# A GEGLU layer with a quantized down projection: the up projection as seven block products a tile instead of eight, its low weight parts streamed

## The chip, the cores and the metric

One Trainium2 chip, one core. The metric is the device time of one execution in microseconds (us). The core has TensorE (PE; its weight loads are shown as PEld), VectorE (DVE), ScalarE (ACT), GpSimd (POOL) and SyncE (SP), which here issues all transfers. Each engine works its own instructions in order; semaphores order the engines among each other.

## The reference

`x` is 4 x 1024 x 512 float32, `cond` 4 x 128, `norm_w` 512 x 128, `up_w` 4096 x 512, `down_w` 512 x 2048.

```python
scale = cond @ norm_w.T + 1.0
ms = jnp.mean(x * x, axis=-1, keepdims=True)
h = x * (scale[:, None, :] * jax.lax.rsqrt(ms + EPS))
val, gate = jnp.split(h @ up_w.T, 2, axis=-1)
h = val * jax.nn.gelu(gate, approximate=False)
y = act_quant(h) @ weight_quant(down_w).T     # h to 255 levels by the row's largest |h|; down_w to -1, 0, 1 by its mean |w|
return y + x
```

## The kernel before

The 4,096 rows of `x` are worked in NB = 8 blocks of TB = 512 rows, the 2,048 hidden columns in J = 16 tiles of 128. All of it is transposed: hidden columns on the partitions, rows of `x` as columns of the matmul. A tile of a block is one step of the up projection. float32 accuracy comes from two float16 parts of each operand, high and low, and three products a pass: high by high, high weight by low x, low weight by high x (lines 257 to 259).

**PE.** `gate` and `val` call `up_half`: 4 slices of the contraction (KT) by 3 products of 512 columns, each into its own bank of `ps_u`. A tile is 24 products. In block b, PE also does the row maxima of block b-1 (`turn_max`, four transposes into `ps_m`), the spread of its scale (`spread_scale`, into `ps_s`), the spread of the next block's reciprocal root (`spread_rs`), and the down products of block b-1 in four groups of 16 (`down`, line 305) after tiles 8 to 11.

**ACT.** `gelu` of the gate bank into `g` (L394), `absolute` of the finished `h` into the same buffer (L400), squares of the next block's rows (L410), x high parts (`high`, L418), and in block 0 `weight_bound` (largest |w| of a tile, L427), `weight_high` (`w_hi`, L432) and `sum_down` (L439).

**DVE.** `hidden` (L612) is `h = val * g`; `peak_of` (L625) keeps the running maximum; `quantize` scales h (L650) and rounds it to `q` (L655); `residual` (L662) scales the down product and adds x; `norm` (L595) and `low` (L602) make the next block's x; `rsqrt` (L564 to L579) is a chain of small operations; in block 0 `weight_scale` (L536 to L546) and `weight_low` (`w_lo`, L553).

**POOL.** Block 0: a reduction over the partitions for each tile's weight scale (L510). Then the quantized down weights `dw` (L524 to L528).

**SP and the transfers.** Up weights come in once, through four stages `w_raw`, and stay on chip in two float16 parts for all tiles, 1,024 columns each a tile. Rows of x stay in `xr`, three blocks deep; the residual is written into them and stored from there.

The order of each engine's work is written out by hand. Block 0 is written out tile by tile, as in this part of DVE's order:

```python
for j in range(J):
    if j + 2 < J:
        weight_scale(j + 2, j % 2)
    if j >= 1:
        peak_of(0, j - 1, (j - 1) % 2, first=True)
    if j + 2 < J:
        weight_low(j + 2, j % 2)
    hidden(0, j, j % 2, first=True)
```

Blocks 1 to 6 are a loop of the hardware, block 7 and the tail are written out again. In the tail `last_down` (L364) goes tile by tile behind the quantization of block 7, which DVE and ACT share (L767, L771, L495, L497).

## Time and profile before

| | |
|---|---|
| median of 3 runs | 814.78 us (814.5 to 814.89) |
| span of the profiled execution | 813.9 us |
| PE busy | 791.4 us |
| PEld busy | 363.4 us |
| DVE busy | 419.8 us |
| ACT busy | 258.8 us |
| POOL busy | 36.4 us |
| moved by DMA | 42.42 MB |

The profile is of one execution; its span is the time from the first to the last instruction, and the table's first row includes what lies around it. Busy is the sum of the durations; PE's matmuls overlap in the profile (each is shown as 0.38 us while one starts each 0.22 us), so the share says where PE is without work, not how fast it is. The chain of work that ended last goes back from the last instruction, at each step to what released it.

### The profile page before, as it was taken

What the parts mean: (1) busy time and instruction counts of PE and PEld (TensorE: products, weight loads), DVE (VectorE), ACT (ScalarE), POOL (GpSimd) and SP (SyncE); (2) the same over time, 40 slices, a digit from 0 to 9 for tenths busy, and PEclk for the clock granted to TensorE, in tenths of its full rate; (3) what the DMA queues carried; (4) which work ended last, traced back from release to release, by engine and by line L of the source; (5) the groups of instructions that cost most, each with busy time, mean ns of one, the idle gap of its engine ahead of it and who ended that gap; (6) DMA issues with size and microseconds to landing.
All of it is one profiled execution on the core that took longest, in us unless ns stands there. A gap on an engine that the chain in (4) does not pass through costs nothing.

```text
span 813.9 us, 12449 instructions
## 1 busy us (share of the span) xinstructions
PE 791.4 (97%) x3688; PEld 363.4 (45%) x3688; DVE 419.8 (52%) x830; ACT 258.8 (32%) x430; POOL 36.4 (4%) x48
## 2 busy tenths in 40 slices
PE   1999999999999999999999999999999999999997
PEld 1444444444444444444444444444444444444443
DVE  4667778433664426743376334664346633563237
ACT  3887623222232122322232221322223222221224
POOL 0100076000000000000000000000000000000000
PEclk9999999999999999999999999999999999999999
DMA  7744530003000030001100030000300010000002
GB/s 271 257 157 155 201 106 4 14 26 117 0 0 13 33 110 0 0 26 60 68 0 0 26 122 7 0 0 26 129 0 0 0 39 13 1 0 14 13 5 74
DMA packets 11825, 42.42 MB, mean 52 GB/s; under 512 B 1440, under 2 KB 1440, under 8 KB 9760
## 3 DMA queue, kind: packets, MB, share of 16 engines
q1 hardware_dynamic: 11808, 42.21, 14.3%
q8 instruction: 8, 0.13, 0.1%
q14 instruction: 9, 0.07, 0.0%
HBM read 33.82 MB, written 8.39 MB: 52 GB/s over the span
## 4 chain that ended last, share of the span: by engine, by line
PE 95%; DVE 3%; issue 1%; ACT 0%; DMA 0%; POOL 0%; SPq 0%; DVEq 0%; ACTq 0%
PE ps_u L257 27%; PE ps_u L258 27%; PE ps_u L259 27%; PE ps_y L305 11%; DVE h L767 1%; PE ps_m L283 1%; PE ps_s L290 0%; PE ps_m L298 0%; PE ps_u L364 0%; DMA scaled<-in_norm_t_dram 0%; DVE w_raw L771 0%; DVE h_max L625 0%; PE ps_y L344 0%; DVE h L612 0%; DVE xr L662 0%
## 5 line engine op out<-in xcount | busy, mean ns | idle before, releaser
L257 PE MATMUL ps_u<-x_hi,w_hi 128*128 (+1 forms) x1024 | 389.1, 380 | 3.4 <-DVE x_lo L602 3.4
L258 PE MATMUL ps_u<-x_lo,w_hi 128*128 (+1 forms) x1024 | 389.1, 380 | 0.0
L259 PE MATMUL ps_u<-x_hi,w_lo 128*128 (+1 forms) x1024 | 389.1, 380 | 0.0
L612 DVE SCALAR_TENSOR_TENSOR h<-ps_u,w_unscale,g 128x512 f32<-128x512 f32 (+1 forms) x128 | 96.0, 750 | 276.0 <-PE ps_u L259 274.6
L400 ACT ACTIVATE g<-h 128x512 f32 (+1 forms) x128 | 80.6, 630 | 335.9 <-DVE h L612 335.9
L257 PEld LDWEIGHTS ps_u<-x_hi,w_hi 128*128 (+1 forms) x1024 | 100.3, 98 | 123.5 <-DVE w_lo L553 3.8
L259 PEld LDWEIGHTS ps_u<-x_hi,w_lo 128*128 (+1 forms) x1024 | 100.4, 98 | 121.5 <-issue 1.1
L258 PEld LDWEIGHTS ps_u<-x_lo,w_hi 128*128 (+1 forms) x1024 | 100.4, 98 | 118.5 <-issue 0.6
L394 ACT ACTIVATE g<-ps_u,w_unscale 128x512 f32<-128x512 f32 x128 | 87.4, 683 | 178.8 <-PE ps_u L259 176.4
L305 PE MATMUL ps_y<-dw,q 128*128 128x512 bf16 x448 | 101.4, 379 | 0.0
L625 DVE TENSOR_TENSOR h_max<-g,h_max 128x512 f32<-128x512 f32 x120 | 83.9, 699 | 32.6 <-ACT g L400 32.6
L650 DVE TENSOR_TENSOR scaled<-h,ps_s 128x512 f32<-128x512 f32 x112 | 71.5, 680 | 10.1 <-PE ps_s L290 10.1
L305 PEld LDWEIGHTS ps_y<-dw,q 128*128 128x128 bf16 x448 | 43.9, 98 | 52.4
L655 DVE TENSOR_SCALAR q<-scaled 128x512 bf16<-128x512 f32 (+1 forms) x112 | 46.6, 459 | 0.0
L602 DVE TENSOR_TENSOR x_lo<-xn,x_hi 128x512 f32 (+1 forms) x32 | 22.0, 691 | 26.9 <-ACT x_hi L418 26.8
L553 DVE SCALAR_TENSOR_TENSOR w_lo<-w_raw,w_scale,w_hi 128x1024 f16<-128x1024 f32 x16 | 20.6, 1284 | 15.5 <-ACT w_hi L432 15.5
L595 DVE SCALAR_TENSOR_TENSOR xn<-xt_raw,cs,ps_m 128x512 f32<-128x512 f32 x32 | 23.5, 740 | 0.7 <-PE ps_m L298 0.7
L432 ACT ACTIVATE w_hi<-w_raw,w_scale 128x1024 f16<-128x1024 f32 x16 | 18.3, 1143 | 14.8 <-DVE w_scale L540 14.8
L662 DVE SCALAR_TENSOR_TENSOR xr<-ps_y,dequant,xr 128x512 f32 (+1 forms) x28 | 20.9, 746 | 2.6 <-PE ps_y L305 2.6
L418 ACT CAST x_hi<-xn 128x512 f32 (+1 forms) x32 | 19.7, 617 | 5.0 <-DVE xn L595 2.8
L427 ACT ACTIVATE q<-w_raw 128x1024 bf16<-128x1024 f32 x16 | 16.7, 1044 | 0.0
L298 PE MATMUL ps_m<-ident,rs 128*128 128x128 f32 x32 | 5.3, 292 | 10.0 <-DVE rs L579 10.0
(62 smaller groups left out, 193.9 us busy)
## 6 DMA issues: line engine op xcount, KB each, us to landing
xr<-in_x_rows_dram SPq DMA_DIRECT2D x8, 1024.0 KB, 6.4
w_raw<-in_up_t_dram SPq DMA_DIRECT2D x16, 512.0 KB, 4.2
xt_raw<-in_x_cols_dram SPq DMA_DIRECT2D x8, 1024.0 KB, 5.4
out_dram<-xr SPq DMA_DIRECT2D x32, 256.0 KB, 2.5
xr<-in_down_t_dram SPq DMA_DIRECT2D x8, 512.0 KB, 4.2
w_raw<-in_down_t_dram SPq DMA_DIRECT2D x8, 512.0 KB, 4.4
scaled<-in_norm_t_dram SPq DMA_DIRECT2D x1, 256.0 KB, 2.8
cond_sb<-in_cond_t_dram SPq DMA_DIRECT2D x1, 2.0 KB, 1.6
```

The source lines that it names most:

```text
L257: pe.matmul(bank, w_hi[:, w_at], x_hi[:, x_at], start=(kt == 0), stop=False)
L258: pe.matmul(bank, w_hi[:, w_at], x_lo[:, x_at], start=False, stop=False)
L259: last = pe.matmul(bank, w_lo[:, w_at], x_hi[:, x_at], start=False, stop=(kt == KT - 1))
L305: last = pe.matmul(ps_y[:, i % 2, :], q[:, j * TB + i * P:j * TB + (i + 1) * P], dw[:, j * D:(j + 1) * D], start=(j == 0), stop=(j == J - 1))
L394: act.activation(g[:, s, :], ps_u[:, 2 * s + 1, :], ACT.Gelu, scale=w_unscale[:, ds(j, 1)]).then_inc(g_ready, 1)
L400: act.activation(g[:, s, :], h[:, ds(j * TB, TB)], ACT.Abs).then_inc(h_abs_ready, 1)
L595: dve.scalar_tensor_tensor(out=xn[:, kt % 2, :], in0=xt_raw[:, kt * TB:(kt + 1) * TB], scalar=cs[:, ds(kt * B + b // PER_B, 1)], in1=ps_m[ ...
L602: dve.tensor_tensor(x_lo[:, at], xn[:, kt % 2, :], x_hi[:, at], ALU.subtract).then_inc(x_lo_ready, 1)
L612: dve.scalar_tensor_tensor(out=h[:, at], in0=ps_u[:, 2 * s, :], scalar=w_unscale[:, ds(j, 1)], in1=g[:, s, :], op0=ALU.mult, op1=ALU.mult) ...
L625: dve.tensor_tensor(h_max[:], g[:, s, :], h_max[:], ALU.max).then_inc(h_max_ready, 1)
L650: dve.tensor_tensor(scaled[:, s, :], h[:, ds((t + s) * TB, TB)], ps_s[:], ALU.mult).then_inc(scaled_ready, 1)
L655: dve.tensor_scalar(q[:, ds((t + s) * TB, TB)], scaled[:, s, :], ROUND, ROUND, ALU.add, ALU.subtract).then_inc(q_ready, 1)
```

## The change

The x block of 512 rows and the contraction of 512 are each halved, and so are the two halves (value and gate) of a weight tile; the 2 x 2 block product is done with Strassen's scheme in Winograd's form: seven block products of 2 slices by 3 passes by 256 columns (`product`), 42 a tile. The operands are A11, A12, A22 and four sums S1 to S4 of weight blocks, and B11, B21, B22 and four differences of x blocks.

- Weight sums: `weight_sums` on POOL, four operations of 128x256, for each tile in block 0. `w_hi` and `w_lo` of a tile are 1,792 columns wide.
- `w_hi` stays on chip for all tiles. `w_lo` is a ring of LS = 4 tiles: written in block 0, stored to DRAM (`store_lo`), and loaded again for each tile of blocks 1 to 7 (`load_lo`, three tiles ahead).
- Two stages instead of four for the up weights (the first lies in `q`) and for the down weights.
- x: `norm` in place in `xt`, four `difference` operations, and seven high and seven low parts of 512 columns where there were four.
- Sums of the products: ACT's `copies` takes the first pair of a tile out of its bank (one half to the gate bank `ps_g`, one to `p5`), DVE's `seed_gate` adds the second product into the gate bank, and `second_val` adds the third into the value bank. Products accumulate on top.
- The order on PE: first pair of tile n; third and both gate products of tile n-1; second of tile n; fourth of tile n-1. So a tile is finished in the step after its own. ACT and DVE follow with hidden, absolute and peak of tile n-2.
- `ps_m` serves maxima, scales and roots alike, `ps_s` is gone; the banks are three for values, two for gates, two for the down product.
- Down products of block b-1: the first group after tile 15 of block b, the other three in tiles 0 to 2 of block b+1. Quantization of a block is spread over tiles 3 to 14 of the next, two, one, one tile of h at a step.
- Rows of x for the squares and for the residual are loaded apart, in pieces of 128 rows, into two buffers each (`xs`, `res`); a result is stored from `res` before the buffer is loaded again.
- All 128 tiles are written out, with no loop of the hardware. `X_TOP` is 2^8 instead of 2^10.

```diff
-            def up_half(b, j, s, which, as_ready=False):
-                    pe.matmul(bank, w_hi[:, w_at], x_hi[:, x_at], start=(kt == 0), stop=False)
-                    pe.matmul(bank, w_hi[:, w_at], x_lo[:, x_at], start=False, stop=False)
-                    last = pe.matmul(bank, w_lo[:, w_at], x_hi[:, x_at], start=False, stop=(kt == KT - 1))
...
+            def load_up(j):
+                if j >= 2:
+                    sp.wait_ge(w_ready, j - 1)
+                sp.dma_start(stage[j % 2][:, 0:WJ], up_t[j]).then_inc(up_loaded[j % 2], 16)
+
+            def store_lo(j):
+                sp.wait_ge(w_ready, j + 1)
+                sp.dma_start(lo_dram[j], w_lo[:, (j % LS) * WO:(j % LS + 1) * WO]).then_inc(lo_stored[j % LS], 16)
+
+            def load_lo(n):
+                j = n % J
+                sp.wait_ge(val_ready, n - LS + 1)
+                sp.wait_ge(lo_stored[n % LS], 16 * (J // LS))
+                sp.dma_start(w_lo[:, (n % LS) * WO:(n % LS + 1) * WO], lo_dram[j]).then_inc(lo_loaded[n % LS], 16)
...
+            def load_res(c, i):
+                u = y_tile(c, i)
+                if u >= 2:
+                    sp.wait_ge(y_stored[u % 2], 16 * (u // 2))
+                sp.dma_start(res[:, u % 2, :], x_rows[c][:, i * D:(i + 1) * D]).then_inc(res_loaded[u % 2], 16)
+
+            def store_y(c, i):
+                u = y_tile(c, i)
+                sp.wait_ge(y_done, u + 1)
+                sp.dma_start(out[c][:, i * D:(i + 1) * D], res[:, u % 2, :]).then_inc(y_stored[u % 2], 16)
...
+                if j == 0 and 1 <= b < NB - 1:
+                    load_xt(b + 1)
+                for c in range(1, NB):
+                    for i in range(TT):
+                        if xs_tile(c, i) >= 2 and n == squares_at(c, i) - 1:
+                            load_xs(c, i)
+                if b >= 1 and j in (12, 13):
+                    load_res(b - 1, j - 12)
+                if b >= 2 and j < 4:
+                    if j in (1, 2):
+                        load_res(b - 2, j + 1)
+                    store_y(b - 2, j)
+                if n + 3 >= J and n + 3 < NJ:
+                    load_lo(n + 3)
+            for i in range(TT):
+                if i in (1, 2):
+                    load_res(NB - 2, i + 1)
+                store_y(NB - 2, i)
+            for i in range(TT):
+                if i < 2:
+                    load_res(NB - 1, i)
+            for i in range(TT):
+                store_y(NB - 1, i)
+                if i < 2:
+                    load_res(NB - 1, i + 2)
+            for k in range(2):
+                sp.wait_ge(y_stored[k], NB * TT // 2 * 16)
...
+            def product(n, op, xop, bank, half, start=False):
+                b, j = divmod(n, J)
+                if j == 0:
+                    pe.wait_ge(x_hi_ready, NOP * b + xop + 1)
+                    pe.wait_ge(x_lo_ready, NOP * b + xop + 1)
+                to = bank[:, half * HB:(half + 1) * HB]
+                for kt in range(2):
+                    wh = ((j * NOP + op) * 2 + kt) * P
+                    wl = (((n % LS) * NOP + op) * 2 + kt) * P
+                    xa = (((b % 2) * NOP + xop) * 2 + kt) * HB
+                    hi, lo = x_hi[:, xa:xa + HB], x_lo[:, xa:xa + HB]
+                    pe.matmul(to, w_hi[:, wh:wh + P], hi, start=start and kt == 0, stop=False, skip_group_check=True)
+                    pe.matmul(to, w_hi[:, wh:wh + P], lo, start=False, stop=False, skip_group_check=True)
+                    last = pe.matmul(to, w_lo[:, wl:wl + P], hi, start=False, stop=(kt == 1), skip_group_check=True)
+                return last
+
+            def first_pair(n):
+                b, j = divmod(n, J)
+                if b == 0:
                     pe.wait_ge(w_ready, j + 1)
+                else:
+                    pe.wait_ge(lo_loaded[n % LS], 16 * ((n - J) // LS + 1))
+                if n >= NV:
+                    pe.wait_ge(h_ready, n - NV + 1)
+                bank = ps_v[:, n % NV, :]
+                product(n, OA11, XB11, bank, 0, start=True)
+                product(n, OS1, XT1, bank, 1).then_inc(pair_ready, 1)
+
+            def second(n):
+                pe.wait_ge(pair_copied, 2 * (n + 1))
+                product(n, OS2, XT2, ps_v[:, n % NV, :], 0).then_inc(u2_ready, 1)
+
+            def third(n):
+                pe.wait_ge(g_seeded, n + 1)
+                product(n, OS3, XT3, ps_v[:, n % NV, :], 0).then_inc(u3_ready, 1)
+
+            def gates(n):
+                bank = ps_g[:, n % NG, :]
+                product(n, OA12, XB21, bank, 0)
+                product(n, OS4, XB22, bank, 1).then_inc(gate_ready, 1)
+
+            def fourth(n):
+                pe.wait_ge(v2_ready, n + 1)
+                product(n, OA22, XN4, ps_v[:, n % NV, :], 0).then_inc(val_ready, 1)
+
+            def spread_rs(c):
+                pe.wait_ge(rs_ready, c + 1)
+                if c >= 1:
+                    pe.wait_ge(xn_ready, c * KT)
+                if c >= 3:
+                    pe.wait_ge(scaled_ready, (c - 2) * J)
+                for i in range(TT):
+                    last = pe.transpose(ps_m[:, i * P:(i + 1) * P], rs[:, i:i + 1].to_broadcast([P, P]), ident[:])
+                last.then_inc(rs_rows, 1)
...
+                pe.wait_ge(xn_ready, min(b + 3, NB) * KT)
+                pe.wait_ge(scaled_ready, b * J)
...
+            for n in range(NJ + 1):
+                b, j = divmod(n, J)
+                if n < NJ:
+                    first_pair(n)
+                if n >= 1:
+                    third(n - 1)
+                    gates(n - 1)
+                if n < NJ:
+                    second(n)
+                if n >= 1:
+                    fourth(n - 1)
+                if n == NJ:
+                    break
+                if 1 <= b and j == 2:
+                    spread_scale(b - 1)
+                for c in range(1, NB):
+                    if n == spread_rs_at(c):
+                        spread_rs(c)
+                if b >= 2 and j < 3:
+                    down(b - 2, j + 1)
+                if b >= 1 and j == J - 1:
+                    down(b - 1, 0)
+                if 1 <= b and j == 1:
+                    turn_max(b - 1)
+
+            down(NB - 2, 1)
+            down(NB - 2, 2)
             turn_max(NB - 1)
+            down(NB - 2, 3)
             spread_scale(NB - 1)
+
+            banks = [ps_v[:, 0, :], ps_v[:, 1, :], ps_v[:, 2, :], ps_g[:, 0, :]]
...
+            def copies(n):
+                act.wait_ge(pair_ready, n + 1)
+                if n >= NG:
+                    act.wait_ge(g_ready, n - NG + 1)
+                act.copy(ps_g[:, n % NG, 0:HB], ps_v[:, n % NV, 0:HB]).then_inc(pair_copied, 1)
+                if n >= 2:
+                    act.wait_ge(v2_ready, n - 1)
+                act.copy(p5[:, n % 2, :], ps_v[:, n % NV, HB:TB]).then_inc(pair_copied, 1)
...
+            for n in range(NJ + 2):
+                b, j = divmod(n, J)
+                if n < NJ:
+                    copies(n)
+                if n >= 2:
+                    absolute(n - 2)
+                if 1 <= n < NJ + 1:
+                    gelu(n - 1)
+                if b == 0:
+                    if j + 2 < J:
+                        weight_high(j + 2)
+                    if j + 3 < J:
+                        weight_bound(j + 3)
+                    if j == 12:
+                        high(1, XB11)
+                        high(1, XT1)
+                        high(1, XT2)
+                    if j == 13:
+                        high(1, XT3)
+                    if j == 14:
+                        high(1, XB21)
+                        high(1, XB22)
+                        high(1, XN4)
+                if 1 <= b < NB - 1:
+                    if j == 2:
+                        high(b + 1, XB11)
+                        high(b + 1, XT1)
+                        high(b + 1, XT2)
+                        high(b + 1, XT3)
+                    if j == 3:
+                        high(b + 1, XB21)
+                        high(b + 1, XB22)
+                        high(b + 1, XN4)
+                for c in range(1, NB):
+                    for i in range(TT):
+                        if n == squares_at(c, i):
+                            square(c, i)
+                if J - 1 <= n < J + 3:
+                    sum_down(2 * (n - J + 1))
+                    sum_down(2 * (n - J + 1) + 1)
...
+            def weight_sums(j):
+                part = [stage[j % 2][:, k * 2 * P:(k + 1) * 2 * P] for k in range(8)]
+                a21, a22, a11, a12, s1, s2, s3, s4 = part
+                pool.wait_ge(up_loaded[j % 2], (j // 2 + 1) * 16)
+                pool.tensor_tensor(s1, a21, a22, ALU.add).then_inc(s_step, 1)
+                pool.tensor_tensor(s3, a11, a21, ALU.subtract).then_inc(s_step, 1)
+                pool.wait_ge(s_step, 4 * j + 1)
+                pool.tensor_tensor(s2, s1, a11, ALU.subtract).then_inc(s_step, 1)
+                pool.wait_ge(s_step, 4 * j + 3)
+                pool.tensor_tensor(s4, a12, s2, ALU.subtract).then_inc(s_step, 1)
...
+            def seed_gate(n):
+                dve.wait_ge(u2_ready, n + 1)
+                dve.tensor_tensor(ps_g[:, n % NG, HB:TB], ps_v[:, n % NV, 0:HB], p5[:, n % 2, :],
+                                  ALU.add).then_inc(g_seeded, 1)
+
+            def second_val(n):
+                dve.wait_ge(u3_ready, n + 1)
+                dve.tensor_tensor(ps_v[:, n % NV, HB:TB], ps_v[:, n % NV, 0:HB], p5[:, n % 2, :],
+                                  ALU.add).then_inc(v2_ready, 1)
...
+            for n in range(NJ + 2):
+                b, j = divmod(n, J)
+                if 1 <= b < NB and j == 2:
+                    row_scales(b - 1)
+                if b == 0 and j + 2 < J:
+                    weight_scale(j + 2)
+                if n >= 2:
+                    hidden(n - 2)
+                if 1 <= n < NJ + 1:
+                    second_val(n - 1)
+                if n >= 2:
+                    peak_of(n - 2)
+                if b >= 2 and j < 4 and n < NJ:
+                    residual(b - 2, j, ps_y[:, j % 2, :])
+                k = j - Q_FIRST
+                tiles = []
+                if 1 <= b < NB and 0 <= k < len(Q_COUNT):
+                    tiles = Q_ORDER[sum(Q_COUNT[:k]):sum(Q_COUNT[:k + 1])]
+                for t in tiles:
+                    scaled(b - 1, t)
+                if n < NJ:
+                    seed_gate(n)
+                for t in tiles:
+                    rounded(b - 1, t, q)
+                if b == 0:
+                    if j + 2 < J:
+                        weight_low(j + 2)
+                    if j == 10:
+                        norm(1, 0)
+                        norm(1, 1)
+                    if j == 11:
+                        norm(1, 2)
+                        norm(1, 3)
+                    if j == 12:
+                        difference(1, XT1)
+                        difference(1, XT2)
+                    if j == 13:
+                        low(1, XB11)
+                        difference(1, XT3)
+                        low(1, XT1)
+                    if j == 14:
+                        difference(1, XN4)
+                        low(1, XT2)
+                        low(1, XT3)
+                    if j == 15:
+                        low(1, XB21)
+                        low(1, XB22)
+                        low(1, XN4)
+                if b == 1 and j == 3:
                     dve.wait_ge(d_summed, ND)
                     dve.tensor_reduce(d_sum[:], d_sums[:], AX.X, ALU.add).then_inc(d_sum_ready, 1)
+                if b == 1 and j == 4:
                     dve.wait_ge(d_total_ready, 1)
                     dve.tensor_scalar(d_mean[:], d_total[:], 1.0 / (J * P * D), CLIP, ALU.mult,
                                       ALU.max).then_inc(d_step, 1)
                     dve.wait_ge(d_step, 1)
                     dve.reciprocal(d_scale[:], d_mean[:]).then_inc(d_scale_ready, 1)
+                if 1 <= b < NB and j == 5:
+                    row_dequant(b - 1)
+                if 1 <= b < NB - 1:
+                    if j == 1:
+                        for kt in range(KT):
+                            norm(b + 1, kt)
+                    if j == 2:
+                        difference(b + 1, XT1)
+                        difference(b + 1, XT2)
+                        low(b + 1, XB11)
+                        difference(b + 1, XT3)
+                        low(b + 1, XT1)
+                        difference(b + 1, XN4)
+                    if j == 15:
+                        for k in (XT2, XT3, XB21, XB22, XN4):
+                            low(b + 1, k)
+                for c in range(1, NB):
+                    if n == rsqrt_at(c):
+                        rsqrt(c)
+
+            residual(NB - 2, 0, ps_y[:, 0, :])
+            residual(NB - 2, 1, ps_y[:, 1, :])
             residual(NB - 2, 2, ps_y[:, 0, :])
+            row_scales(NB - 1)
+            row_dequant(NB - 1)
+            residual(NB - 2, 3, ps_y[:, 1, :])
             for j in range(J):
+                scaled(NB - 1, j)
                 if j % 2 == 1:
+                    rounded(NB - 1, j - 1, q_last)
+            banks = [ps_v[:, 0, :], ps_v[:, 1, :], ps_v[:, 2, :], ps_g[:, 0, :]]
             for i in range(TT):
...
```

## Rows read from the trace of the kernel before

**Rows 1.** The page: busy time by engine, and the chain that ended last by engine

```profile
PE 791.4 (97%) x3688; PEld 363.4 (45%) x3688; DVE 419.8 (52%) x830; ACT 258.8 (32%) x430; POOL 36.4 (4%) x48
...
PE 95%; DVE 3%; issue 1%; ACT 0%; DMA 0%; POOL 0%; SPq 0%; DVEq 0%; ACTq 0%
```

**Rows 2.** Windows of block 0 and the tail: stretch, its us, busy us of each engine

```profile
20.30:106.40 86.10, 86.09 (x389) 38.59 (x390) 57.66 (x133) 65.32 (x105) 7.18 (x18) 1.00 0.51 183
786.90:813.90 27.00, 22.30 (x105) 10.07 (x103) 19.44 (x37) 10.71 (x17) 0.00 (x0) 1.00 0.16 59
```

**Rows 3.** The chain in order of time: start us, us, what

```profile
154.94 3.45 PE ps_y L305 x16
...
305.89 0.65 PE ps_m L283 x4
...
404.14 0.65 PE ps_m L283 x4
...
793.17 1.29 DVE h L767 x2
```

**Rows 4.** Timeline of PE and its weight loads around a group of transposes

```profile
443.70 0.57 PEld L298 LDWEIGHTS ps_m<-ident,rs 128*128 128x128 f32 x4
443.92 0.60 PE L298 MATMUL ps_m<-ident,rs 128*128 128x128 f32 x4
...
444.36 0.38 PE L257 MATMUL ps_u<-x_hi,w_hi 128*128 x1
```

**Rows 5.** The page's groups of instructions: xcount | busy us, mean ns | idle before, releaser

```profile
L612 DVE SCALAR_TENSOR_TENSOR h<-ps_u,w_unscale,g 128x512 f32<-128x512 f32 (+1 forms) x128 | 96.0, 750 | 276.0 <-PE ps_u L259 274.6
L400 ACT ACTIVATE g<-h 128x512 f32 (+1 forms) x128 | 80.6, 630 | 335.9 <-DVE h L612 335.9
L257 PEld LDWEIGHTS ps_u<-x_hi,w_hi 128*128 (+1 forms) x1024 | 100.3, 98 | 123.5 <-DVE w_lo L553 3.8
...
L394 ACT ACTIVATE g<-ps_u,w_unscale 128x512 f32<-128x512 f32 x128 | 87.4, 683 | 178.8 <-PE ps_u L259 176.4
...
L625 DVE TENSOR_TENSOR h_max<-g,h_max 128x512 f32<-128x512 f32 x120 | 83.9, 699 | 32.6 <-ACT g L400 32.6
...
L553 DVE SCALAR_TENSOR_TENSOR w_lo<-w_raw,w_scale,w_hi 128x1024 f16<-128x1024 f32 x16 | 20.6, 1284 | 15.5 <-ACT w_hi L432 15.5
...
L432 ACT ACTIVATE w_hi<-w_raw,w_scale 128x1024 f16<-128x1024 f32 x16 | 18.3, 1143 | 14.8 <-DVE w_scale L540 14.8
```

**Rows 6.** Timeline of DVE and ACT: a reciprocal root, and one tile of block 0

```profile
13.34 0.17 DVE L564 TENSOR_SCALAR ms<-sumsq 128x4 f32<-128x4 f32 x1
...
15.61 0.15 DVE L536 TENSOR_SCALAR peak_all<-peak_all 128x1 f32<-128x1 f32 x1
...
38.29 1.28 DVE L553 SCALAR_TENSOR_TENSOR w_lo<-w_raw,w_scale,w_hi 128x1024 f16<-128x1024 f32 x1 [1.46 <-ACT w_hi L432]
...
39.50 0.74 DVE L612 SCALAR_TENSOR_TENSOR h<-ps_u,w_unscale,g 128x512 f32<-128x512 f32 x1
...
41.85 1.13 ACT L432 ACTIVATE w_hi<-w_raw,w_scale 128x1024 f16<-128x1024 f32 x1
...
43.08 1.28 DVE L553 SCALAR_TENSOR_TENSOR w_lo<-w_raw,w_scale,w_hi 128x1024 f16<-128x1024 f32 x1 [1.45 <-ACT w_hi L432]
```

**Rows 7.** POOL: its group of reductions, and two single operations of the timeline

```profile
L510 POOL PARTITION_ALL_REDUCE peak_all<-peak x16 | 6.3, 391 | 78.0 <-ACT q L427 78.0
...
105.19 1.10 POOL L524 TENSOR_SCALAR w_raw<-w_raw,d_scale 128x1024 f32<-128x1024 f32 x1 [9.58 <-issue]
...
123.08 1.80 POOL L524 TENSOR_SCALAR w_raw<-w_raw,d_scale 128x1024 f32<-128x1024 f32 x1
```

**Rows 8.** The page's DMA issues: xcount, KB each, median us from issue to landing

```profile
w_raw<-in_up_t_dram SPq DMA_DIRECT2D x16, 512.0 KB, 4.2
...
out_dram<-xr SPq DMA_DIRECT2D x32, 256.0 KB, 2.5
...
scaled<-in_norm_t_dram SPq DMA_DIRECT2D x1, 256.0 KB, 2.8
```

718 lines of the change are left out of this document (319 added, 399 removed).

## The prediction

> **What bounds the kernel now.** I read the summary by engine first. TensorE is busy 97% of the span, and the chain that ended last lies on PE for 95% [rows 1]. So PE's own instructions, their number and their spacing, make the time. The windows cut the 813.9 us into three pieces: 20.3 us before the first up product, 766.6 us up to 786.9, where the last up product ends (block 0 is 86.1 of them, up to 106.4, and blocks 1 to 7 are the other 680.5), and a tail of 27.0 us [rows 2]. The chain in order of time gives the spacing: sixteen down products of 512 columns take 3.45 us, 0.2157 us each, and from one block's transposes of the row maxima to the next block's are 98.25 us [rows 3]. That is 384 up products (82.83 us), 64 down products (13.80) and 1.6 us of transposes with their gaps. Nothing else fits in: in the middle blocks PE never waits. DVE is busy 52% and ACT 32% [rows 1], so they have room, but not without limit.
>
> **Fewer columns.** A tile had 24 products of 512 columns and gets 42 of 256: 12,288 columns become 10,752. The catch is that each product still loads 128x128 weights, and there are now 5,376 of them where there were 3,072. At 2.4 GHz 512 columns are 0.2133 us, so 0.0024 us of the 0.2157 is a fixed part of each product; 256 columns are then 0.1067 + 0.0024 = 0.1091 us. A load takes 0.098 us [rows 5] and starts with the product ahead of it, so it would just be covered. The nearest row: four transposes with a load each start at 443.92 and the next product at 444.36, 0.11 us a pair, loads included [rows 4]. I take 0.1091. The bounds: half of 0.2157, 0.1078 (7 us less in all); 0.11 from the transposes (5 us more); and load and stream one after the other, 0.206, which those transposes make unlikely. A tile costs 42 x 0.1091 = 4.58 us instead of 5.18, and 128 tiles save 76 us if nothing else is late. The rest of the working is what is late.
>
> The Trainium skill, "TensorE: Matmul & The Clock Gate", sections on the wait of 56 ns and on the back-to-back gap, has a fixed 2.5 ns per product, which the trace's 0.2157 agrees with. The same page says that pairs of load and product do not get below 81 ns, which would leave my 0.109 alone, but also that the sequencer, when it decodes in software, spends 62 ns per matmul; if a load costs it the same, a pair is 0.124 us and the sum 80 us higher. The pair of 0.11 in the trace speaks against it, over four pairs only.
>
> **One tile in the new order.** From the tile's start on PE (0): first pair to 1.31, third and gates of the tile before to 3.27, second to 3.93, fourth of the tile before to 4.58. An operation of 256 columns isn't in the trace. DVE's 512 columns take 0.70 to 0.75, ACT's 0.63 to 0.68, and the 1,024-column rows give 1.04 and 1.03 ns a column [rows 5]; so 256 columns are 0.45 on DVE and 0.38 on ACT (bounds: half and the whole of the 512-column rows). ACT copies at 1.68 to 2.4, wanted at 3.27. `second_val` goes at 2.33 to 2.8, wanted at 3.93. `seed_gate` waits for second (4.30), ends near 4.75, and in a tile in which two tiles are quantized, near 5.45; wanted by third at 5.89. So steady tiles don't stall, by a margin of 0.4 us.
>
> **Places that stall, blocks 1 to 7.** A Newton reciprocal root is eleven small operations, from 13.34 to 15.61: 2.3 us [rows 6]. Where it comes in a tile without a down product (j=11, blocks 1 to 5), DVE is 0.9 us late for the next seed; j=3 with a residual costs 0.2. So 1.1 us in blocks 2 to 6. Block 1 has no down products in its first tiles to hide things: `spread_rs(2)` waits for a root queued behind that tile's seed (2.7), `turn_max(0)` for four norms of 0.66 each behind the next seed (2.9), and at tile 19 the copies stand on ACT behind four x copies and two sums of down chunks of 1.14 us each [rows 5] (2.6); with the small ones 9.4. All blocks together: 9.4 + 5.5 + 0.2 = 15.1 us. The low parts of the weights, 0.46 MB a tile, take about the 4.2 us of an up load [rows 8] and have two tiles, 9.2 us; I cost them at nothing. That cover is gone only if SyncE stands still for 4 us, which in blocks 2 to 7 I don't find.
>
> **Block 0.** Here the price is. The first product starts at about 21 (20.3 before [rows 2]; the same chain of scales and the root leads to it, with one difference, 0.6, and a low part 0.8 longer on DVE, and squares moved from DVE to ACT, 1.3 less; the rest I round up). What is prepared per tile is 1,792 columns instead of 1,024, in two stages instead of four. ACT's `w_hi` goes from 1.14 to 1.94 us, DVE's `w_lo` from 1.28 to 2.08 [rows 5]. The queues are in order, so this closes a ring (an operation starts up to 0.1 before the one ahead of it ends: `w_lo` at 38.29 takes 1.28, hidden starts at 39.50 [rows 6]): DVE `w_lo` ends; the four scale operations (0.57); hidden (0.75); hand-over (0.12); ACT absolute (0.53); gelu (0.57); `w_hi` 1.94; hand-over (0.10); `w_lo` 2.00 to the next. 6.58 us a tile, against 4.58 on PE and 4.79 from one `w_lo` to the next before, 38.29 to 43.08, `w_hi` ending at 42.98 [rows 6]. A second ring is the stage: load 4.2 [rows 8] plus issue 0.3, `weight_bound` 1.14 (priced as the 1,024 columns of `w_hi`), the reduction over partitions 0.5, gives 6.2: just inside (the reduction itself is 0.39, with hand-overs 0.5 [rows 7]). A third is POOL: four sums of 128x256 after that reduction have 2.9 us until `w_hi` wants them. POOL has no two-input row here; one-input 128x1024 takes 1.10 to 1.80 [rows 7], so a sum is between 0.26 (a quarter) and 1.8. I take 0.5, nearest to the quarter but for two inputs: 2.3 with hand-overs, inside. Since `w_lo` and the POOL sums both read SBUF, and POOL's 1.80 against 1.10 stands beside a working DVE, I add 0.2: 6.8 a tile. At the upper end the sums would add 4.6 a tile, 55 us.
>
> The Trainium skill, "GPSIMD Engine Reference", section on elementwise cycle accounting, gives 4,497 ns for a two-input sum of 2,048 elements; an estimate from that page is 0.56 for 256, and the sum above would stay at 6.8. "SBUF — State Buffer", section "Who interferes with whom", has DVE with two SBUF inputs and GpSimd exclude each other; the trace's 1.80 against 1.10 agrees.
>
> Until the ring runs: two norms, three differences and five low parts (each 0.6 to 0.7) come between the first `w_lo` and the second, so the low part of tile 1 is done at 30.2, of tile 2 at 34.9, of tile 3 (its load waits for tile 1, ACT loads a table) at 42.5. Twelve more at 6.8 are 81.6; the root of x block 1, its four norms and first two differences on the same DVE queue add 2.3 + 2.6 + 1.2. Low part of tile 15: 130.2. Tile 16 starts 8.5 later: 138.7. Before, it was 106.4.
>
> **Tail.** Three groups of down products, 3.45 us each, stand behind the last up product instead of two, and `res` has two buffers. Residual (6,2) waits for a store (2.5) and a load (2.8) [rows 8], then `row_scales` and residual (6,3): the first `scaled` comes 13.3 us after the last product, not 6.2 (793.17 [rows 3] less 786.9); one residual (0.66) is no longer among them. At the very end the rows of (7,2) and (7,3) are loaded only after the stores of (7,0) and (7,1), and SyncE takes them in order: store, load, store, load, store is 12.0 us from the first residual where it was 5.5. So 27.0 + 7.1 - 0.7 + 6.5 = 39.9.
>
> **Sum.** 138.7 to tile 16. Then seven blocks of 16 x 4.58 (513.2), the last third, gates and fourth (2.6), 25 groups of down products (86.3), transposes and their gaps as before (11.0: 680.5 less 579.8 and 26 groups of 3.45), stalls 15.1: 628.2 instead of 680.5. Tail 39.9. 806.8 us of span. The run of before has 814.78 with a span of 813.9, so 0.9 more: 807.7. Saved in blocks 1 to 7: 52; given back: 32 in block 0, 13 in the tail.
>
> **Rivals.** A, the sum as it stands (800 to 813): 0.40. B, block 0 or the stalls are cheaper, as the ring is not closed in each tile (say 6.2 a tile and half the stalls: 793): 0.18. C, the other side: POOL's sums end behind the 2.9 us and the ring is longer. It decides from 7.4 us a tile (7.1 us over 12 tiles); at 8.0 a tile, 822. For it the 1.80 rows, against it the idle POOL: 0.17. D, the steady tiles stall: the margin of 0.4 us is used up by PSUM-to-PSUM operations, which no row shows, and 0.25 us in each of 112 tiles gives 836: 0.10. E, the pair of load and product isn't 0.109: each ns is 5.4 us, so from 0.1104 on the change is slower; at 0.12, 866. Against it the transposes: 0.05. No change that can be told (0.2%, 1.6 us, is about what this kernel's runs can tell): 0.10.
>
> From these: faster 0.58, same 0.10, slower 0.32. The likeliest case's own range is 800 to 813. The range for 8 in 10 leaves out the far ends of POOL's price and of the pair: 790 to 842.
>
> **What would show it.** Starts of up products 0.109 apart; low parts in block 0 6.8 apart, with `w_hi` released by `w_scale` and absolute by hidden, not by POOL; tile 16 at 139; blocks 2 to 6 89.9 us from one turn of the maxima to the next; last up product at 767; tail 40. A released-by-POOL in `w_hi` is C; PE idle before second or third in ordinary tiles is D.

## The result, and the profile after

The changed kernel takes 965.12 us (964.06 to 965.7, 4 runs); beside it the kernel before took 814.84 (814.5 to 815.76). The ratio is 1.184, with an interval of 1.1825 to 1.1859: 18% slower, where 1% faster was forecast. The profiled execution of the changed kernel has a span of 963.3 us, 156.5 more than the 806.8 of the prediction's sum. Two executions that ran at a lower granted clock, one of the kernel before (938.33 us) and one of experiment 7 (982.07 us), are left out of all that follows.

The page after, against [rows 1]: busy time by engine, TensorE's granted clock in 40 slices, and the chain that ended last by engine.

```profile
PE 762.0 (79%) x5966; PEld 607.0 (63%) x5994; DVE 563.0 (58%) x1138; ACT 356.3 (37%) x714; POOL 80.6 (8%) x113
...
PEclk9967676767678999999999999999999999999998
...
PE 60%; issue 23%; POOL 5%; DVE 5%; ACT 3%; DMA 3%; SPq 0%; POOLq 0%; ACTq 0%; DVEq 0%
```

No engine is near its limit any more. The new thing is "issue" with 23% of the chain: time in which the engine on the chain waited for nothing that the profile shows. 23% of 963 is some 220 us. Next, where it lies. Three windows after, cut at the first up product, the start of tile 16, the end of the last up product and the end of the span (stretch, us, busy us of PE, PEld, DVE, ACT, POOL, then the granted clock):

```profile
27.30:288.20 260.90, 115.14 (x652) 80.48 (x653) 85.66 (x170) 80.82 (x132) 47.68 (x75) 0.71 0.24 74
288.20:920.80 632.60, 616.06 (x5186) 511.82 (x5210) 448.04 (x902) 255.67 (x550) 28.20 (x25) 0.99 0.41 132
920.80:963.30 42.50, 26.94 (x119) 12.09 (x119) 20.86 (x39) 10.94 (x18) 0.00 (x0) 0.88 0.27 87
```

| piece | before [rows 2] | predicted | after | after less predicted |
|---|---|---|---|---|
| up to tile 16's first product | 106.4 | 138.7 | 288.2 | +149.5 |
| from there to the end of the last up product | 680.5 | 628.2 | 632.6 | +4.4 |
| tail | 27.0 | 39.9 | 42.5 | +2.6 |

So blocks 1 to 7 and the tail came as forecast, within 1% and 7%, and all but 7 us of the miss lies before tile 16. There PE is busy for 44% of the time, DVE for 33% and POOL for 18%. What ended the waits is in the table of waits of the whole program (us in total, times, longest); nearly all of these lie in block 0:

```profile
PE ps_v L378 <- ACT p L523: 115.6, 17, 12.3
DVE w_lo L716 <- issue: 109.6, 12, 9.7
POOL peak_all L672 <- issue: 90.5, 15, 6.6
...
ACT w_hi L576 <- POOL q L667: 71.5, 8, 14.9
ACT w_hi L576 <- POOL stage L667: 63.9, 8, 11.0
...
POOL q L662 <- issue: 59.7, 8, 9.1
POOL stage L662 <- issue: 58.4, 8, 7.9
```

Read it from the end back to the engine that holds the others up: PE's product `second` waits for ACT's copies, the copies stand in ACT's queue behind `w_hi`, and `w_hi` waits 135.4 us in all for POOL's last sum (L667). That is what the prediction had named as the mark of rival C. But POOL isn't busy. It is itself released by "issue": 15 waits of 6.0 us before the reductions (L672) and 16 of 7.4 before the first sum of a tile (L662). One tile in POOL's timeline:

```profile
137.03 0.71 POOL L662 TENSOR_TENSOR stage<-stage 128x256 f32<-128x256 f32 x1 [7.89 <-issue]
137.72 0.71 POOL L663 TENSOR_TENSOR stage<-stage 128x256 f32<-128x256 f32 x1
...
139.19 0.72 POOL L667 TENSOR_TENSOR stage<-stage 128x256 f32<-128x256 f32 x1
145.87 0.38 POOL L672 PARTITION_ALL_REDUCE peak_all<-peak  x1 [5.96 <-issue]
153.94 0.71 POOL L662 TENSOR_TENSOR q<-q 128x256 f32<-128x256 f32 x1 [7.69 <-issue]
```

Four sums (2.9), 5.96 of nothing, a reduction (0.38), 7.69 of nothing: 16.9 us from tile to tile (16.7 on average over the fifteen steps of the program), and that closes without any other engine. The waits stand only where the kind of work changes. Between sums there is none.

The word "issue" alone proves little. DVE's `w_lo` has 109.6 us of it too, and there it is ACT's `w_hi`, which ends 0.1 us before `w_lo` starts:

```profile
140.01 1.79 ACT L576 ACTIVATE w_hi<-stage,w_scale 128x1792 f16<-128x1792 f32 x1 [8.28 <-POOL stage L667]
141.88 2.08 DVE L716 SCALAR_TENSOR_TENSOR w_lo<-stage,w_scale,w_hi 128x1792 f16<-128x1792 f32 x1 [9.66 <-issue]
```

POOL's operands, in contrast, were there: the maximum that the reduction at 145.87 reads was finished on ACT at 142.84, 3.0 us earlier, and the weights that the sum at 153.94 reads had been read by ACT from 141.70 on. In the kernel before, the reductions followed one another and were released by ACT for 78.0 us [rows 7], which looks like idleness; but at the two places where the kind changes, its table of waits has the same thing:

```profile
POOL peak_all L510 <- ACT q L427: 78.0, 15, 8.8
POOL w_raw L524 <- issue: 9.6, 1, 9.6
POOL peak_all L513 <- issue: 9.0, 1, 9.0
```

L524 is the first scaling of the down weights, behind the last reduction, and its row with [9.58 <-issue] stands in [rows 7]: I took the 1.10 of it and passed over the 9.58. L513 is the first reduction, behind an `affine_select`.

### The profile page after: what moved, and what is told of

The parts are those of the page before. It is cut to its first block, busy times and chain, and to the rows that moved or that the text cites. A ratio compares the mean times of both kernels' runs of the same rounds, so it can differ in the third digit from the quotient of the medians.

```text
span 963.3 us, 15408 instructions
## 1 busy us (share of the span) xinstructions
PE 762.0 (79%) x5966; PEld 607.0 (63%) x5994; DVE 563.0 (58%) x1138; ACT 356.3 (37%) x714; POOL 80.6 (8%) x113
## 4 chain that ended last, share of the span: by engine, by line
PE 60%; issue 23%; POOL 5%; DVE 5%; ACT 3%; DMA 3%; SPq 0%; POOLq 0%; ACTq 0%; DVEq 0%
PE ps_v L378 12%; PE ps_v L380 12%; PE ps_v L379 12%; PE ps_y L444 9%; PE ps_g L379 5%; PE ps_g L380 5%; PE ps_g L378 5%; ACT q L570 2%; DMA out_dram<-res 1%; PE ps_v L494 1%; DVE h L832 1%; DMA res<-in_x_rows_dram 1%; POOL peak_all L672 1%; POOL q L667 1%; POOL q L662 1%
## 5 line engine op out<-in xcount | busy, mean ns | idle before, releaser
L378 PE MATMUL ps_v<-x_hi,w_hi 128*128 128x256 f16 x1280 | 368.7, 288 | 162.1 <-ACT p L523 115.6
L379 PE MATMUL ps_v<-x_lo,w_hi 128*128 128x256 f16 x1280 | 368.7, 288 | 0.0
L380 PE MATMUL ps_v<-x_hi,w_lo 128*128 128x256 f16 x1280 | 368.2, 288 | 0.0
L378 PEld LDWEIGHTS ps_v<-x_hi,w_hi 128*128 128x128 f16 x1280 | 131.5, 103 | 197.4 <-ACT p L523 120.6
L380 PEld LDWEIGHTS ps_v<-x_hi,w_lo 128*128 128x128 f16 x1280 | 132.4, 103 | 21.5
L379 PEld LDWEIGHTS ps_v<-x_lo,w_hi 128*128 128x128 f16 x1280 | 131.7, 103 | 22.1
L378 PE MATMUL ps_g<-x_hi,w_hi 128*128 128x256 f16 x512 | 139.9, 273 | 0.0
L379 PE MATMUL ps_g<-x_lo,w_hi 128*128 128x256 f16 x512 | 139.9, 273 | 0.0
L380 PE MATMUL ps_g<-x_hi,w_lo 128*128 128x256 f16 x512 | 139.7, 273 | 0.0
L797 DVE SCALAR_TENSOR_TENSOR h<-ps_v,w_unscale,g 128x512 f32<-128x512 f32 x128 | 95.5, 746 | 3.0 <-PE ps_v L380 2.8
L780 DVE TENSOR_TENSOR ps_g<-ps_v,p 128x256 f32<-128x256 f32 x128 | 55.0, 429 | 14.7 <-PE ps_v L380 8.0
L716 DVE SCALAR_TENSOR_TENSOR w_lo<-q,w_scale,w_hi 128x1792 f16<-128x1792 f32 x8 | 16.7, 2085 | 72.2 <-issue 54.5
L716 DVE SCALAR_TENSOR_TENSOR w_lo<-stage,w_scale,w_hi 128x1792 f16<-128x1792 f32 x8 | 16.7, 2084 | 71.8 <-issue 55.1
```

Source lines behind the costliest of these rows:

```text
L378: pe.matmul(to, w_hi[:, wh:wh + P], hi, start=start and kt == 0, stop=False, skip_group_check=True)
L379: pe.matmul(to, w_hi[:, wh:wh + P], lo, start=False, stop=False, skip_group_check=True)
L380: last = pe.matmul(to, w_lo[:, wl:wl + P], hi, start=False, stop=(kt == 1), skip_group_check=True)
L780: dve.tensor_tensor(ps_g[:, n % NG, HB:TB], ps_v[:, n % NV, 0:HB], p5[:, n % 2, :], ALU.add).then_inc(g_seeded, 1)
L797: dve.scalar_tensor_tensor(out=h[:, at:at + TB], in0=ps_v[:, n % NV, :], scalar=w_unscale[:, j:j + 1], in1=g[:, n % 3, :], op0=ALU.mult, o ...
```

## The experiments

The theory, S: each change of kind on POOL, between a PARTITION_ALL_REDUCE and a tensor operation, costs 6 to 8 us whatever the size of either, and two changes a tile set the length of block 0. Its main rival is the prediction's C in its own form: the sums are long, or are held up by DVE on SBUF. Four kernels separate these.

**1. The sums on DVE, POOL with reductions alone.** `weight_sums` moves from POOL's queue to DVE's:

```diff
@@ pool
-            def weight_sums(j): ...
             for j in range(J):
-                weight_sums(j)
                 weight_peak_all(j)
@@ dve, ahead of weight_low(j + 2)
+                        weight_sums(j + 2)
```

> The changed kernel with the four weight sums of each tile on DVE instead of POOL, nothing else. Theory S (POOL pays 6 to 8 us each time that its work goes from a sum to a reduction over the partitions or back): POOL now does reductions only, the gaps ahead of them vanish, DVE gets four operations of 0.4 us more a tile, so 8.3 us a tile in block 0 instead of 16.9; about 836 us. Rival R (each reduction over the partitions costs 6 us by itself once POOL has a long queue): the 6 us gap stays, some 13 us a tile, about 910 us. Rival W (two stages and 1,792 columns hold block 0, whatever POOL does): stays at about 960 us.

Measured: 836.6 us, ratio 1.027 (1.024 to 1.029), 128 us less than the changed kernel. POOL's reductions are released by ACT again, and the low parts are 8.11 us apart:

```profile
63.27 1.25 POOL L661 PARTITION_ALL_REDUCE peak_all<-peak  x1 [6.85 <-ACT q L570]
...
62.23 2.08 DVE L715 SCALAR_TENSOR_TENSOR w_lo<-stage,w_scale,w_hi 128x1792 f16<-128x1792 f32 x1 [1.27 <-issue]
...
70.34 2.08 DVE L715 SCALAR_TENSOR_TENSOR w_lo<-q,w_scale,w_hi 128x1792 f16<-128x1792 f32 x1 [1.27 <-issue]
```

This moves both the work and the changes of kind off POOL, so it doesn't yet tell S from long sums. It does show that the ring of the prediction is what is left when POOL's part is gone: its 6.58, without the 0.2 for POOL beside DVE, and the four sums on DVE's queue (1.46 us, from 65.13 to 66.59) are 8.04.

**2. The reductions off POOL, the sums on it.** PE transposes the broadcast column of peaks (as `spread_rs` does) into a bank of `ps_y`, and DVE reduces its 128 columns:

```diff
@@ pe
+            def spread_column(column, ready, count, slot, done):
+                pe.wait_ge(ready, count)
+                pe.transpose(ps_y[:, slot, 0:P], column.to_broadcast([P, P]), ident[:]).then_inc(done, 1)
@@ dve, at the head of weight_scale(j)
+                dve.wait_ge(ready, count)
+                dve.tensor_reduce(to, ps_y[:, slot, 0:P], AX.X, op).then_inc(done, 1)
@@ pool
-                weight_peak_all(j)
```

> The changed kernel with every reduction over the partitions (the scale of cond, 16 weight peaks, the sum of the down weights) taken from POOL and done by a PE transpose of the broadcast column and a DVE reduction of 128 columns; the sums stay on POOL at 0.71 us each. Theory S: no change of kind is left, about 7 us a tile in block 0, tile 16 at 140 us instead of 288, total about 815 us (812 to 825). Rival T (the two-input sums need 7 us ahead of them on POOL by themselves): the gap of 7 us stays ahead of the sums, about 12 us a tile, 880 to 900 us. Rival W: about 960 us.

Measured: 823.69 us, ratio 1.0105 (1.008 to 1.013), a span of 821.5. The expectation was 815 (812 to 825). POOL does the same sixty-four sums as in the changed kernel, and 141 us are gone. So it wasn't the sums' size. POOL's rows, and two low parts 7.27 us apart:

```profile
64.39 1.62 POOL L683 TENSOR_TENSOR stage<-stage 128x256 f32<-128x256 f32 x1 [3.54 <-DMA stage<-in_up_t_dram]
65.97 0.72 POOL L684 TENSOR_TENSOR stage<-stage 128x256 f32<-128x256 f32 x1
...
63.34 2.08 DVE L732 SCALAR_TENSOR_TENSOR w_lo<-q,w_scale,w_hi 128x1792 f16<-128x1792 f32 x1 [1.27 <-issue]
...
70.61 2.08 DVE L732 SCALAR_TENSOR_TENSOR w_lo<-stage,w_scale,w_hi 128x1792 f16<-128x1792 f32 x1 [1.27 <-issue]
```

The first sum is now released by the DMA, and is the only long one of this tile: 1.62 us where the next takes 0.72. From 63.34 to 65.42 `w_lo` runs on DVE. In other tiles it is another of the four that is long, up to 2.51.

**3. The kernel before, with one small sum behind each reduction.** This has none of the change: no Strassen, no sums of weights. The sum is of one column and nothing uses it.

```diff
             for j in range(J):
                 weight_peak_all(j)
+                pool.tensor_tensor(tiny[:, j:j + 1], ident[:, 0:1], ident[:, 1:2], ALU.add)
```

> The kernel before with one sum of 128x1 on POOL behind each of the 16 weight reductions, its result unused. Theory S: the size does not matter, only that the kind changes twice a tile: 6.0 + 0.4 + 7.3 + 0.2, about 14 us a tile in block 0 instead of 5.4; about 950 us. If the price lay in the size of the sums, the two stages or the wide parts: 815 us, as before.

Measured: 958.64 us, ratio 1.176 (1.174 to 1.179). Sixteen operations of 0.18 us, 2.9 us of work in all, make the kernel before 144 us longer (about 135 were expected; two of the waits before a reduction were 7.8 and 9.7):

```profile
65.00 0.18 POOL L518 TENSOR_TENSOR tiny<-ident 128x1 f32<-128x1 f32 x1 [7.19 <-issue]
71.17 0.38 POOL L511 PARTITION_ALL_REDUCE peak_all<-peak  x1 [5.98 <-issue]
79.22 0.18 POOL L518 TENSOR_TENSOR tiny<-ident 128x1 f32<-128x1 f32 x1 [7.68 <-issue]
85.25 0.38 POOL L511 PARTITION_ALL_REDUCE peak_all<-peak  x1 [5.84 <-issue]
```

**4. The changed kernel with its sums cut to one column.** The four sums write one column each; the rest of the sums' part of the stage holds a constant, so the products of those parts aren't those of the reference.

```diff
                 part = [stage[j % 2][:, k * 2 * P:(k + 1) * 2 * P] for k in range(8)]
+                part = [t[:, 0:1] for t in part]
```

> The changed kernel with each of the four weight sums cut to one column of 256; the rest of the sum blocks holds a constant, so the result is not the reference's. Theory S: only the work of the sums goes, 2.8 us down to about 0.6, 14.6 us a tile; about 930 us. If the sums' own work on POOL were the price: block 0 near the 6.8 us a tile of the prediction, about 810 us.

Measured: 929.2 us, ratio 1.140 (1.138 to 1.142). The size of the sums is worth 36 us of the changed kernel's 965, 2.2 us a tile: (0.71 - 0.18) x 4 is 2.1. The waits are as long as before:

```profile
63.80 0.18 POOL L664 TENSOR_TENSOR stage<-stage 128x1 f32<-128x1 f32 x1 [7.26 <-issue]
...
70.29 0.38 POOL L674 PARTITION_ALL_REDUCE peak_all<-peak  x1 [5.74 <-issue]
78.23 0.18 POOL L664 TENSOR_TENSOR q<-q 128x1 f32<-128x1 f32 x1 [7.56 <-issue]
```

With 3 and 4 the price is measured in two kernels and for sums of 1 and of 256 columns: 5.7 to 6.0 us toward the reduction, 7.2 to 7.9 toward the sum in these rows. The wait before a reduction is also the same whether its operand comes late or early: in the changed kernel the maximum is there 2.9 us behind POOL's last sum, in 3 it was there (61.17) 4.0 us before the sum ended (65.18), and the reduction starts 5.96 and 5.98 us behind the sum. S stands, and "long sums" falls.

**5 to 7. What the design is worth without the changes of kind.** Three kernels start from number 2 and go after the two other terms that the prediction had priced: the loads in the tail, and the ring of block 0.

Number 5 loads the rows of x for the last six residuals during block 7, into `xs` and `xt`, which are free by then:

```diff
+            def load_early(c, i):
+                k = y_tile(c, i) - EARLY
+                if k < 2:
+                    sp.wait_ge(sumsq_ready, NB * TT)
+                else:
+                    sp.wait_ge(x_lo_ready, NOP * NB)
+                sp.dma_start(home(c, i), x_rows[c][:, i * D:(i + 1) * D]).then_inc(early_loaded[k], 16)
...
+                if b == NB - 1 and 5 <= j < 11:
+                    u = EARLY + j - 5
+                    load_early(u // TT, u % TT)
```

> The kernel with its reductions off POOL (823.7 us, span 821.5), and in it the rows of x for the last six residuals are loaded during block 7 into tiles that are free by then: (6,2) and (6,3) into the two xs tiles, (7,0) to (7,3) into xt. So no residual waits for a store and a load. T (the terms of the tail as the prediction put them: the last residual no longer two stores and two loads behind, 12.0 back to 5.5 us, and the first scaled about 2 us sooner, since the third residual of block 6 no longer waits for its rows while the third group of down products still does): tail 42.7 - 8.7 = 34, time 815 us (813 to 817). Rival N (the waits on the loads cover something else that is as late: the stores at the end take their time anyway): 821 us or more.

Number 6 opens the ring: a third stage, on ACT `weight_high` and `weight_bound` ahead of `absolute` and `gelu`, on DVE `peak_of` behind `weight_low`, and on PE the peak spread right behind the first pair (not in the lines shown).

```diff
-        stage = [stage0, stage1[:]]
+        stage = [stage0, stage1[:], h[:, 12 * TB:16 * TB]]
@@ act, tile n of block 0
+                    weight_high(j + 2)
+                    weight_bound(j + 3)
                     absolute(n - 2)
                     gelu(n - 1)
-                    weight_high(j + 2)
-                    weight_bound(j + 3)
@@ dve, tile n of block 0
-                    peak_of(n - 2)
                     ...
                     weight_low(j + 2)
+                    peak_of(n - 2)
```

> The kernel with its reductions off POOL, and in block 0: a third stage of raw weights (in the part of h for tiles 12 to 15, which is written only after tile 14's weights are done), each load one tile earlier; ACT does w_hi and the bound of the next tile ahead of absolute and gelu; DVE takes peak_of behind w_lo; PE spreads the peak right behind the first pair. All the instructions stay. R (block 0 is a ring of load and queue order, as the sum of the prediction had it, once POOL no longer changes its kind of work): a tile is then bound by the busier of ACT (copies 0.72, w_hi 1.8, bound 1.25, absolute and gelu 1.3: 5.1 us) and DVE (scales 0.9, hidden 0.75, three of 0.43 to 0.7, w_lo 2.08: 5.3 us), 5.5 us with hand-overs instead of 7.27; over 13 tiles 23 us less: 801 us (797 to 808). Rival N (block 0 is bound by POOL's four sums beside DVE, by DMA or by TensorE's lower clock there): at least 7.0 a tile, 819 to 824.

Number 7 has both edits.

> Both edits: the new order and third stage in block 0, and the rows for the tail early. If they are independent, the time is 823.7 less the sum of what each saves alone: about 792 us (787 to 799), ratio to the kernel before 0.972. If the reductions and the tail were all that stood between the prediction and the change, this is the design as its author could have had it: 52 us saved in blocks 1 to 7, block 0 about 12 us longer than before, tail 7 longer.

| kernel | time, us | ratio to before, interval |
|---|---|---|
| 5, rows early | 812.16 | 0.9967 (0.9957 to 0.9977) |
| 6, third stage and order | 809.2 | 0.9928 (0.991 to 0.9946) |
| 7, both | 796.57 | 0.9768 (0.9747 to 0.9789) |

Number 5 came 1 us below its range, 7 inside its own. 5 saves 11.5 us and 6 saves 14.5; 823.7 less both is 797.7, so the two edits don't get in each other's way. The tail term holds, and a little more than it: in 5 the last up product ends at 777.2 of a span of 808.8, which leaves 31.6 us where number 2 had 42.4 (the expectation's 42.7 puts the last product 0.3 early), so 10.8 less where 8.7 were expected. The last residuals now wait for PE, not for a load. DVE's timeline at the end, of the changed kernel first and of 7 below it:

```profile
929.72 0.75 DVE L847 SCALAR_TENSOR_TENSOR res<-ps_y,dequant,res 128x512 f32<-128x512 f32 x1 [4.51 <-DMA res<-in_x_rows_dram]
...
934.46 1.28 DVE L832 TENSOR_TENSOR h<-h,ps_m 128x512 f32<-128x512 f32 x2
...
949.25 1.61 DVE L847 SCALAR_TENSOR_TENSOR res<-ps_v,dequant,res 128x512 f32<-128x512 f32 x2 [2.46 <-PE ps_v L494]
955.77 0.75 DVE L847 SCALAR_TENSOR_TENSOR res<-ps_v,dequant,res 128x512 f32<-128x512 f32 x1 [4.91 <-DMA res<-in_x_rows_dram]
959.84 0.75 DVE L847 SCALAR_TENSOR_TENSOR res<-ps_g,dequant,res 128x512 f32<-128x512 f32 x1 [3.32 <-DMA res<-in_x_rows_dram]
```

```profile
789.00 2.48 DVE L880 SCALAR_TENSOR_TENSOR xt<-ps_v,dequant,xt 128x512 f32<-128x512 f32 x3 [1.47 <-PE ps_v L529]
791.59 0.75 DVE L880 SCALAR_TENSOR_TENSOR xt<-ps_g,dequant,xt 128x512 f32<-128x512 f32 x1
```

Number 6 missed its expectation by 8 us: 801 were expected, within 797 to 808. Tile 16 starts at 133.1, 16.4 us earlier than in number 2, where 23 were expected. Its first tiles do what was expected of them, and so do those of 7, where the low parts are 5.4 to 6.3 us apart between 52.0 and 80.8. DVE in 7:

```profile
57.90 2.08 DVE L746 SCALAR_TENSOR_TENSOR w_lo<-q,w_scale,w_hi 128x1792 f16<-128x1792 f32 x1 [0.46 <-issue]
...
63.27 2.08 DVE L746 SCALAR_TENSOR_TENSOR w_lo<-stage,w_scale,w_hi 128x1792 f16<-128x1792 f32 x1 [0.46 <-issue]
...
80.79 2.09 DVE L746 SCALAR_TENSOR_TENSOR w_lo<-stage,w_scale,w_hi 128x1792 f16<-128x1792 f32 x1 [0.46 <-issue]
...
83.93 0.69 DVE L755 TENSOR_SCALAR ms<-sumsq 128x4 f32<-128x4 f32 x1
...
91.78 2.09 DVE L746 SCALAR_TENSOR_TENSOR w_lo<-h,w_scale,w_hi 128x1792 f16<-128x1792 f32 x1 [0.20 <-issue]
```

Behind 80.8 the same DVE queue takes the start of x block 1: the root, four norms and two differences, while ACT gets its first x copies. The expectation had spread 5.5 us over all 13 tiles; from tile 10's low part (80.79) to tile 15's (121.19) it is 8.1 a tile. The root itself takes 5.2 us, from 83.93 to 89.1, where [rows 6] had 2.3 for the same operations (they are twelve, not the prediction's eleven): six of them, of 128x4 elements, last 0.56 to 0.69 instead of 0.16, while POOL's sums run. So DVE was the bound there, as named, with work on it that the estimate had left out.

Three windows of 7; the first is cut at 144.0, 11 us behind the start of tile 16:

```profile
21.40:144.00 122.60, 92.78 (x746) 76.15 (x747) 103.88 (x206) 87.46 (x149) 50.05 (x52) 0.96 0.56 172
144.00:763.20 619.20, 606.18 (x5104) 503.96 (x5128) 440.24 (x881) 248.02 (x533) 27.94 (x24) 0.99 0.42 133
763.20:795.10 31.90, 25.73 (x122) 11.86 (x122) 20.85 (x39) 11.28 (x18) 0.00 (x0) 0.99 0.18 67
```

DVE is busy 103.9 of the first 122.6 us (95.8 of the 111.5 up to tile 16), so I expect little more from block 0 without moving work off it; no run tried. Tile 16 starts at 132.9 (26.5 later than before), the last up product ends at 763.5 (23.4 earlier), and the tail is 4.6 longer: 18.8 us of span gained, of the 50 that blocks 1 to 7 give.

## Why the prediction was wrong

**The step that failed** is in the paragraph on block 0: "A third is POOL: four sums of 128x256 after that reduction have 2.9 us until `w_hi` wants them." The sums were priced by their size, between 0.26 and 1.8 us, and the reductions by theirs, 0.39. The order on POOL, reduction, sums, reduction, sums, had no price at all. It costs 6.0 + 7.4 us a tile, so POOL's own ring is 16.7 us and not inside the 6.8. From the end of tile 1's low part to that of tile 15's are 234.5 us (42.8 to 277.3) where the prediction had 100.0 (30.2 to 130.2, with 6.1 for x block 1). The same price (6.78 us before the first sum, then 6.11 and 6.84) stands in the way of the start: the first product is at 27.3, not 21 (21.4 in number 7, without reductions on POOL), and tile 1's low part is 12.6 behind its time. Together with 2.4 us from there to tile 16 that is the 149.5. The bound from above, 1.8 us a sum, could not have held it either, since it was again a size. Rival C had the engine and the sign (0.17), and 8.0 us a tile as its price.

**What number 2 leaves of the miss.** With the changes of kind gone the span is 821.5, 14.7 above the sum. Tile 16 starts at 149.5 there, 10.8 late: the low part of tile 15 ends at 140.5 (130.2 predicted), that of tile 3 at 44.4 (42.5), so twelve tiles took 96.1 us where 81.6 and 6.1 for x block 1 were taken. In the tile shown in 2 the pitch from `w_lo` to `w_lo` is 7.27, not 6.8. Two things in it are not in the prediction's ring. DVE reduces 128 columns (0.29), which belongs to number 2's own way of taking the maximum. And it waits 0.55 for that maximum, because `weight_bound` on ACT has waited 1.09 for the raw weights: the ring of the stage, put "just inside", binds in this tile too. The middle is 1.4 over, the tail 2.5. So the ring was right in kind (6.65 in number 1, 8.11 less the sums) and too short in size once loads are late. With number 2's way of reducing, the kernel is 1% slower, by the measured 823.7, not 1% faster; what it would be with reductions on POOL at no price no run shows.

**The pitch of 0.1091** was right. Three starts in the middle of the changed kernel; the 41 steps from 295.57 to 300.04 are 0.1090 each:

```profile
601.04 0.27 PE L380 MATMUL ps_g<-x_hi,w_lo 128*128 128x256 f16 x1
601.15 0.27 PE L378 MATMUL ps_g<-x_hi,w_hi 128*128 128x256 f16 x1
601.26 0.27 PE L379 MATMUL ps_g<-x_lo,w_hi 128*128 128x256 f16 x1
```

Rival E falls, as in the full blocks nothing is left for the loads: 88.86 us less 13.80 for the down products and 1.6 for the transposes are 73.5 for 672 products, 0.1093 each. With it falls what the prediction made of the 62 ns per matmul in the Trainium skill, "TensorE: Matmul & The Clock Gate", section on the wait of 56 ns: a pair of load and product at 0.124 is in no full block of this trace. The 81 ns that the prediction takes from that page as a floor of all pairs stands there for products of 128 columns; nothing in the sum rests on it.

**The steady tiles** don't stall (rival D falls): DVE's PSUM sums take 0.43 us (0.45 taken), ACT's copies 0.36 (0.38), and from 420 to 760 us PE waits 0.8 us in all for `seed_gate`. The chain in order of time has the transposes of the maxima 88.86 us apart in full blocks (89.9 predicted, 98.25 before [rows 3]):

```profile
306.84 1.09 PE ps_m L427 x4
...
402.90 0.44 PE ps_m L427 x4
...
491.76 0.44 PE ps_m L427 x4
```

The 1.1 us for a late root in blocks 2 to 6 were not spent, 5 us in all, and the stretch is still 4.4 over. So block 1 cost some 9 us more than the 9.4 (worked out as the rest). The trace has what makes it up. Before the first of these transposes PE waits 6.5 us where 2.9 were predicted, because the norms ahead of them on DVE wait 3.88 for their rows of x, a load priced at nothing:

```profile
304.01 2.72 DVE L751 SCALAR_TENSOR_TENSOR xt<-xt,cs,ps_m 128x512 f32<-128x512 f32 x4 [3.88 <-DMA xt<-in_x_cols_dram]
```

At 340.76 ACT's squares have waited 5.54 for theirs, and PE waits 3.03 for the copies behind them, which was not in the sum at all. Behind each of these two waits the granted clock is at its lower level for 3 to 5 us (0.53 from 307 to 312): the transposes take 0.88 up to the next product instead of 0.44, and 18 and 15 products start 0.21 apart (307.72, 307.93) instead of 0.11, 1.9 and 1.6 us. That is 3.6 + 3.0 + 0.4 + 3.5 = 10.5 us more; the root and the copies at tile 19 came 0.6 and 0.5 under their prices (2.1 for 2.7, 2.1 for 2.6), which leaves 9.4.

**The tail** was 42.5 for 39.9. The first `scaled` comes 13.7 us after the last product (13.3 predicted). From the first of the last residuals (949.25) to the end of the span are 14.05 us, where store, load, store, load, store had been put at 12.0.

**The conversions** were near: `w_hi` 1.79 (1.94), `w_lo` 2.08 (2.08), a load of low parts 3.4 us, waited for once, by 0.3 us, so to cost it at nothing was right.

## What to carry to other kernels

Price the order on an engine as well as the size of its operations: look in the trace of before for an "issue" wait at each place where that engine changes its kind of work, and multiply it by the changes that the edit adds. An engine that is 4% busy is no free engine if what it does is of another kind than what it is given. And where a design moves its cost into a first stage and a tail, work those two out before the gain: here blocks 1 to 7 gave 48 to 51 us in the changed kernel, in 2 and in 7, and what lies before and behind them decided between +18% and -2.3%.

## What the runs showed of the hardware

- On POOL a PARTITION_ALL_REDUCE behind tensor operations starts 5.7 to 6.6 us after the last of them (two in experiment 3 by 7.8 and 9.7), and a TENSOR_TENSOR or TENSOR_SCALAR behind a reduction 6.7 to 7.9, with single ones of 8.5 to 9.8 among the first three of a program. The first reduction of a program stands 9.0 to 10.6 us behind the operation ahead of it; in the kernel before 4.4 and in the changed one 5.9 of them come after its operand was there. It doesn't depend on the size (1 or 256 columns), and operations of one kind follow one another without it. The profile counts 17 packets on the two instruction queues in the kernel before and 18 in experiment 3, which has some thirty such waits more, so it records no load of instructions for them; no run here shows what the engine does meanwhile.
- A two-input sum of 128x256 in f32 takes POOL 0.71 us alone, one of 128x1 0.18: a fixed part and 2.1 ns a column. The Trainium skill, "GPSIMD Engine Reference", section on elementwise cycle accounting, led to an estimate of 0.56, since its figure for 2,048 columns was scaled without a fixed part. Beside a DVE operation single sums took 0.9 to 2.5.
- It goes the other way too: DVE operations of 128x4 elements took 0.56 to 0.69 us instead of 0.16 while POOL summed, each ending with a POOL operation (84.65 + 0.65 on DVE, 84.56 + 0.72 on POOL). The prediction had from the Trainium skill, "SBUF — State Buffer", section "Who interferes with whom", that DVE with two SBUF inputs and GpSimd exclude each other; the trace agrees. The running maximum (128x512) took 1.22 instead of 0.68 there, so both lose about half a microsecond, and small operations the most for their size.
- TensorE's granted clock was 0.71 in block 0 of the changed kernel, where PE stood idle for more than half of the time, and 0.96 up to 144.0 us in number 7, where it was busy 76%. At the lower level (1.2 GHz) products of 256 columns start 0.21 us apart, at the higher (2.4 GHz) 0.11. While POOL was the bound this cost nothing; in block 1 it cost some 4 us.
